# Causal grouped-query attention in a decoder kernel: scores taken twice, exponentials not transposed, sums of exponentials by additions and a product with ones

## The reference, cut to what matters

```python
q = (x @ Wq + bq).reshape(b, s, NQ, D); k = (x @ Wk + bk).reshape(b, s, NKV, D); v = (x @ Wv + bv).reshape(b, s, NKV, D)
q = _rotary(q); k = _rotary(k)
logits = jnp.einsum('bqhgd,bkhd->bhgqk', q.reshape(b, s, NKV, g, D), k) * scale
logits = jnp.where(causal, logits, jnp.float32(-1e+30))
w = jax.nn.softmax(logits, axis=-1)
out = jnp.einsum('bhgqk,bkhd->bqhgd', w, v).reshape(b, s, NQ * D)
return out @ Wo + bo
```

## Time and profile before

| | |
|---|---|
| median of three runs | 1377.93 us |
| profiled execution: its span, first to last instruction (it has no other time) | 1376.4 us |
| the changed stage, first to last scores | 350.4 to 948.4 us |
| TensorE busy in it | 582.84 of 598.00 us |
| VectorE, ScalarE, GpSimd busy in it | 323.18, 353.64, 193.77 us |
| mean granted TensorE clock, whole span | 0.939 of 2.4 GHz |

### The profile page before, as it was taken

One profiled execution on the slowest core, in us unless ns is written; L12 is line 12 of the kernel. 1 busy time (PEld: TensorE's weight loads), 2 busy tenths in 40 slices (PEclk: granted clock), 3 DMA queues, 4 the chain that ended last, 5 costly groups with the idle time before them and its releaser, 6 DMA issues. The chain is left out here.

```text
span 1376.4 us, 24979 instructions
## 1 busy us (share of the span) xinstructions
PE 1186.4 (86%) x8059; PEld 868.3 (63%) x8060; DVE 865.8 (63%) x1528; ACT 763.2 (55%) x2082; POOL 586.3 (43%) x616
## 2 busy tenths in 40 slices
PE   7888589676899999999999999999898439999991
PEld 4544367455566767777666777776676337888881
DVE  2588799874345545665355555675688666777773
ACT  2498447434555656666455565664366245565652
POOL 1155447656445331431553322200267415666663
PEclk9999789888699999999999999999999658999996
DMA  9100000001010010000100000100730232232325
GB/s 300 40 1 1 0 1 2 1 16 31 17 32 16 16 26 10 14 16 6 42 16 17 16 17 1 47 2 1 269 99 1 74 122 43 46 52 47 50 46 138
DMA packets 42136, 58.27 MB, mean 42 GB/s; under 512 B 6608, under 2 KB 34640, under 8 KB 42032
## 3 DMA queue, kind: packets, MB, share of 16 engines
q1 hardware_dynamic: 34544, 46.70, 11.3%
q0 software_dynamic: 7488, 10.23, 4.6%
HBM read 32.80 MB, written 13.63 MB: 34 GB/s over the span
## 5 line engine op out<-in xcount | busy, mean ns | idle before, releaser
L2016 DVE TENSOR_REDUCE ga_neg_top<-ps 128x1 f32<-128x128 f32 (+7 forms) x256 | 182.0, 753 | 195.2 <-PE ps L1786 194.8
L1897 ACT ACTIVATE ga_e<-ps,ga_neg_top 128x128 f32<-128x128 f32 (+7 forms) x256 | 188.4, 744 | 7.6 <-DVE ga_neg_top L2016 6.8
L1906 ACT COPY ga_e_tr<-ps 128x512 f32<-128x512 f32 (+3 forms) x192 | 92.2, 480 | 174.4 <-PE ps L1795 171.7
L1795 PE MATMUL ps<-ident,ga_e 128*128 128x128 f32 x1152 | 165.1, 278 | 0.9 <-DVE ga_e_tr L2024 0.8
L1811 PE MATMUL ps<-ga_e_tr,ga_v 128*64 128x256 f32 x1152 | 151.7, 391 | 4.1 <-ACT ga_att L1914 4.1
L1795 PEld LDWEIGHTS ps<-ident,ga_e 128*128 128x128 f32 x1152 | 123.3, 142 | 28.0 <-ACT ga_e L1897 14.7
L2024 DVE COPY ga_e_tr<-ps 128x128 f32<-128x128 f32 (+3 forms) x192 | 105.9, 552 | 35.1 <-PE ps L1795 34.8
L1971 POOL TENSOR_TENSOR ga_q_lo<-shared,ga_q_hi 128x1024 fp32r<-128x1024 f32 x15 | 35.6, 2370 | 176.1 <-ACT ga_q_hi L1887 176.1
L2566 DVE TENSOR_TENSOR ex_w_lo<-ex_gate_up,ex_w_hi 128x1024 fp32r<-128x1024 f32 x78 | 92.4, 1226 | 26.6 <-ACT ex_w_hi L2426 26.4
L1811 PEld LDWEIGHTS ps<-ga_e_tr,ga_v 128*64 128x64 f32 x1152 | 72.5, 136 | 49.0 <-issue 23.4
L2426 ACT CAST ex_w_hi<-ex_gate_up 128x1024 fp32r x78 | 77.9, 1046 | 23.7 <-issue 16.4
(11 more groups left out here) (330 smaller groups left out, 2721.4 us busy)
## 6 DMA issues: line engine op xcount, KB each, us to landing
shared<-shared SPq DMA_DIRECT2D x80, 128.0 KB, 2.3
ex_gate_up<-in_ex_gate_up SPq DMA_DIRECT2D x1, 8192.0 KB, 24.3
ex_down<-in_ex_down SPq DMA_DIRECT2D x1, 4096.0 KB, 35.7
x_tr<-in_x_tr SPq DMA_DIRECT2D x4, 512.0 KB, 7.0
x_nat<-in_x SPq DMA_DIRECT2D x1, 2048.0 KB, 11.7
gated_rows<-shared SPq DMA_DIRECT2D x8, 256.0 KB, 2.2
gated_rows<-x_tr SPq DMA_DIRECT2D x8, 256.0 KB, 2.3
x_tr<-summed_rows SPq DMA_DIRECT2D x8, 256.0 KB, 5.1
```

Source lines behind the costliest of these rows:

```text
L1795: last = nc.tensor.transpose(ps_tr[n % 2][:, (kb - k0) * P:(kb - k0 + 1) * P], e[half][t % 2][:, kb * P:(kb + 1) * P], core.ident[:])
L1897: nc.scalar.activation(e[half][t % 2][:, 0:blocks(t) * P], ps_scores(t, half), ACT.Exp, bias=neg_top[t % 2][:, half:half + 1], accum_out=s ...
L1906: nc.scalar.copy(e_tr[g % 2][:, k0:k1, half, t % 2 * P:(t % 2 + 1) * P], ps_tr[n % 2][:, 0:(k1 - k0) * P].rearrange("p (k t) -> p k t", t= ...
L2016: nc.vector.tensor_reduce(neg_top[t % 2][:, half:half + 1], ps_scores(t, half), AX.X, ALU.max, negate=True).then_inc(top_ready, 1)
```

## The change

The stage's ticks stay (now from -10 to 136), but inside them the work is cut anew. A **unit** takes, for a tile two places ahead (tile 1 aside), the scores queries x keys of the high parts only, up to 512 columns a half, adds the mask on the diagonal, and VectorE reduces it (up to 128x1024) to the negated maxima; there are 2, 4, 8, 8, 16, 16, 16, 16 units for n = 1 to 8. Once a tile the maxima are transposed (`turn_top`) and ScalarE writes them four times, masked (`spread_shift`). A **step** (J, c, kb) takes the scores again as keys x queries, for one block of 128 keys, four pairs of heads at once (512 columns): first a product that puts minus the maximum in every row, then the three split products, then on the diagonal the mask; there are 144 steps. ScalarE's exp of a step is one 128x1024 instruction; its output goes into `weigh_values` as it is. The exponentials of a group's steps are added up by VectorE (`add_keys`, 128x1024, 112 of them), and `sum_keys` multiplies the total with a [128, 64] matrix of ones (32 of them), which gives the sums already spread. VectorE inverts [128, 512] of them straight from bank 7 and multiplies. Queries are projected one tile earlier (three buffers), and one key piece at tick 8 instead of 16. On TensorE the work at the end of a tick stands in this order: output projection, transposed output, `turn_top`, `sum_keys`, query pieces, key pieces, value pieces. On ScalarE `spread_shift` follows the exponentials of its tick. The constants (`pair_rows`, `top_rows`, `ones`, `mask_k`) are made in the stage before.

```diff
-        self.recip_rows = sb("recip_rows", [P, P], F32R)
-        self.pick = sb("pick", [P, QT, 2, HD], F32R)
+        self.top_rows = sb("top_rows", [P, KV_PAIRS + R])
+        self.pair_rows = sb("pair_rows", [P, KV_PAIRS, P], F32R)
+        self.ones = sb("ones", [P, HD])
+        self.neg_top = [sb(f"neg_top{i}", [P, 2, HD]) for i in range(2)]
...
+    AHEAD, DRAIN = 10, 9
+    TICKS = range(-AHEAD, TICK_COUNT + DRAIN)
+    Q_BUFFERS, E_BUFFERS = 3, 4
+    steps = [(J, c, kb) for J in range(TILES) for c in range(KV_PAIRS) for kb in range(blocks(J))]
+    for s, (J, c, kb) in enumerate(steps):
+        place = (s - first_step[J]) * QT // (KV_PAIRS * blocks(J))
+        steps_at.setdefault(J * QT + place, []).append(s)
...
+    for J in range(TILES):
+        n_rows = max(1, PIECE // blocks(J))
+        own = [(J, c, r, r + n_rows, n) for c in range(KV_PAIRS) for r in range(0, R, n_rows) for n in range((blocks(J) - 1) // PIECE + 1)]
+        for i, unit in enumerate(own):
+            place = (J - 2) * QT + 6 + i * QT // len(own)
+            if J == 1:
+                place = 2 + i
...
-        return (J + 2, i - 6) if i >= 6 and J + 2 < TILES else None
-    K_STEPS = {1: 2 * QT, 2: 5 * QT, 3: 8 * QT}
+        return (J + 3, i - 6) if i >= 6 and 2 <= J + 3 < TILES else None
+    K_STEPS = {1: QT, 2: 5 * QT, 3: 8 * QT}
...
+    def top_turn_at(t):
+        J, i = divmod(t, QT)
+        return J + 1 if i == 6 and 0 <= J + 1 < TILES else None
+    def sums_at(t):
+        J, i = divmod(t, QT)
+        if i == 6 and 0 <= J < TILES:
+            return J * KV_PAIRS
+        if i == 1 and 1 <= J <= TILES:
+            return (J - 1) * KV_PAIRS + 1
+        return None
...
+                def top_scores(u):
...
+                    need(pe, top_ready, u)
+                    for r in range(r0, r1):
+                        for half in range(2):
+                            last = nc.tensor.matmul(ps_top[:, half, columns], q_hi[J % Q_BUFFERS][rows, c * R + r, :],
+                                                    k_hi[k_slot(b, n)][rows, c, 0:width], start=(r == r0), stop=(r == r1 - 1 and not diagonal))
+                    if diagonal:
+                        for half in range(2):
+                            whole = ps_top[:, half, 0:(r1 - r0) * width].rearrange("p (r k) -> p r k", k=width)
+                            last = nc.tensor.matmul(whole[:, :, width - P:width], ident_bf[:], mask_q[:].unsqueeze(1).to_broadcast([P, r1 - r0, P]),
+                                                    start=False, stop=True)
+                def turn_top(J):
+                    take_piece_bank((shift_ready, J + 1))
+                    pe.wait_ge(top_ready, last_unit[J] + 1)
+                    nc.tensor.transpose(ps_piece[:, 0:P], neg_top[J % 2][:].rearrange("p h x -> p (h x)"), core.ident[:]).then_inc(top_turned, 1)
+                def key_scores(s):
...
+                    need(pe, e_ready, s - 1)
...
+                    for half in range(2):
+                        last = nc.tensor.matmul(out(half), pair_rows[rows, c, :], shift[J % 2][rows, :, :], start=True, stop=False)
+                    for i, (ks, qs) in enumerate(((k_hi, q_hi), (k_hi, q_lo), (k_lo, q_hi))):
+                        for half in range(2):
+                            last = nc.tensor.matmul(out(half), ks[slot][rows, c, keys], qs[J % Q_BUFFERS][rows, heads, :],
+                                                    start=False, stop=(i == 2 and not diagonal))
+                    if diagonal:
+                        for half in range(2):
+                            last = nc.tensor.matmul(out(half), ident_bf[:], mask_k[:].unsqueeze(1).to_broadcast([P, R, P]), start=False, stop=True)
+                def weigh_values(s):
...
+                    pe.wait_ge(e_ready, s + 1)
...
+                    for half in range(2):
+                        last = nc.tensor.matmul(ps_att[half * HD:(half + 1) * HD, :], v[:, v_slot(b, kb), kv * HD:(kv + 1) * HD],
+                                                e[s % E_BUFFERS][:, half, :], start=(kb == 0), stop=(kb == j))
+                def sum_keys(g):
+                    take_piece_bank((recip_ready, g + 1))
...
+                    for half in range(2):
+                        last = nc.tensor.matmul(ps_piece[half * HD:(half + 1) * HD, :], ones[:], of_keys[:, half, :], start=True, stop=True)
...
+                for t in TICKS:
+                    for i in range(max(len(own_steps), len(own_units))):
+                        if i < len(own_steps):
+                            key_scores(own_steps[i])
+                        if i < len(own_units):
+                            top_scores(own_units[i])
+                        if i < len(own_steps) and own_steps[i] >= 1:
+                            weigh_values(own_steps[i] - 1)
...
+                    if top_turn_at(t) is not None:
+                        turn_top(top_turn_at(t))
+                    if sums_at(t) is not None:
+                        sum_keys(sums_at(t))
+                    if q_piece_at(t) is not None:
+                        take_piece_bank((piece_copied, piece["q", *q_piece_at(t)] + 1))
+                        front.pe_project_q(*q_piece_at(t), ps_piece)
...
+                def spread_shift(J):
+                    for r in range(R):
+                        last = nc.scalar.activation(shift[J % 2][:, r, :], ps_piece[:, 0:P], ACT.Copy, scale=top_rows[:, KV_PAIRS + r:KV_PAIRS + r + 1])
...
+                def exponentials(s):
...
+                    nc.scalar.activation(e[s % E_BUFFERS][:], ps_keys[s % 2], ACT.Exp).then_inc(e_ready, 1)
...
+                def find_maximum(u):
...
+                    nc.vector.tensor_reduce(out, ps_top[:, :, 0:(r1 - r0) * width].rearrange("p h (r k) -> p h r k", k=width),
+                                            AX.X, ALU.max, negate=True).then_inc(top_ready, 1)
...
+                def add_keys(s):
+                    before = e[(s - 1) % E_BUFFERS] if kb == 1 else added[g % 2]
+                    nc.vector.tensor_tensor(added[g % 2][:], before[:], e[s % E_BUFFERS][:], ALU.add).then_inc(add_ready, 1)
+                def normalise(g):
+                    dve.wait_ge(sums_ready, g + 1)
+                    nc.vector.reciprocal(recip[:], ps_piece).then_inc(recip_ready, 1)
+                    nc.vector.tensor_tensor(values, values, recip[:], ALU.mult).then_inc(att_done, 1)
...
+                    if sums_at(t - 1) is not None:
+                        normalise(sums_at(t - 1))
+                    for i in range(max(len(own_steps), len(own_units))):
+                        if i < len(own_steps) and own_steps[i] >= 1:
+                            add_keys(own_steps[i] - 1)
+                        if i < len(own_units):
+                            find_maximum(own_units[i])
```

More of the change, by code:

```diff
@@ L1624, in k_slot, with group, ends_group @@
+    def group(s):
+        return steps[s][0] * KV_PAIRS + steps[s][1]
+    def ends_group(s):
+        J, c, kb = steps[s]
+        return kb == blocks(J) - 1
+    adds_through = [sum(kb >= 1 for _, _, kb in steps[:s + 1]) for s in range(len(steps))]
+    tops_merged = [sum(blocks(i) > PIECE for i in range(J + 1)) for J in range(TILES)]
     def k_slot(b, n):
@@ new lines, in exponentials @@
+                def exponentials(s):
+                    act.wait_ge(s_ready, s + 1)
+                    before = s - E_BUFFERS
+                    if before >= 0:
+                        J, c, kb = steps[before]
+                        act.wait_ge(weighed, before + 1)
+                        if blocks(J) == 1:
+                            act.wait_ge(sums_ready, group(before) + 1)
+                        else:
+                            act.wait_ge(add_ready, adds_through[before + 1 if kb == 0 else before])
+                    nc.scalar.activation(e[s % E_BUFFERS][:], ps_keys[s % 2], ACT.Exp).then_inc(e_ready, 1)
@@ L2060, in _ @@
+                    if t == TICK_COUNT:
+                        add_keys(len(steps) - 1)
                         dve.wait_ge(q_lo_ready, TILES)
```

379 lines of the change are left out of this document (149 added, 230 removed).

## The result

The changed kernel takes **1566.86 us** (median of four runs, 1564.7 to 1569.02), the kernel before 1378.12 beside it (1376.24 to 1379.14). The ratio is **1.1376, 95% interval 1.136 to 1.1393**: slower by 188 us. The forecast was 1503 with a range of 1425 to 1570: right in direction and just inside the range, 64 us short.

What follows compares the result with a forecast made beforehand. TensorE's own work was taken as the bound, any new wait paid in full: -10 + 67 + 11 + 25 + 25 + 13 + 10 = +141, less 16 for overlaps, on 1376.4 gives 1501, as a median 1503 us; range 1425 to 1570.

Steps and rivals of the forecast that it cites:

- TensorE's work: Matmuls and transposes removed (308 us) against those added (300) in the stage: -8, taken as -10 us, bounds -25 to +5.
- (a): Tick 6, bank 7: `sum_keys` waits for ScalarE's copies, 20 us; 13 query pieces wait for the reciprocal, 47; sum 67.
- (b): Three key pieces at ticks 0 and 1 wait 3.65 us each at bank 7: 11 us.
- (c): Tick after `sum_keys`: VectorE does reciprocal and product before addition and maximum, stopping TensorE's units: 25 us in about ten tiles.
- (d): VectorE's two-SBUF-input additions contend with GpSimd instructions: 83 us of VectorE, 25 us put on TensorE (0 to 80).
- (e): Stage start: tile 0 needs its maxima first; about 17 us pass, +13 us net (8 to 18).
- (f): Half-clock stretches on TensorE after waits of 3.65 us: 1.7 us each, six of 13 charged, 10 us (0 to 25).
- (g): Constants made in the stage before, and the shorter drain: nothing, 1 us if not.
- Rival 3: TensorE's clock stays low long after each wait, 13 times 4 us lost: 1555 us; chance 0.12.
- Rival 2: VectorE becomes the bound, the GpSimd lock falling on each addition: 1546 us; chance 0.2.
- rival 1: VectorE's reciprocal of 512 columns is as fast as the multiplication (0.69 us): 1430 us; chance 0.08.
- Rival 4: Waits at bank 7 vanish and only TensorE's work counts, so the kernel is faster: 1363 us; chance 0.06.

Runs made afterwards that it cites:

- fillers: Changed kernel plus 14 bf16 products of 512 columns on TensorE behind `sum_keys` at tick 6, ahead of the query piece: 1537 us.
- kernel with a copy: Changed kernel with VectorE's reciprocal of the sums replaced by a copy of the same shape, the inversion left out: 1481 us.
- later pieces: Changed kernel with query pieces one tick later (ticks 7 and 0 instead of 6 and 7): 1568 us.
- late reciprocal: Changed kernel with the sums copied out of bank 7 by ScalarE and inverted by VectorE behind the tick's maxima and additions: 1540 us.
- halves: Changed kernel with copied sums inverted on VectorE in two 256-column parts over two ticks, maxima ahead of additions, turned maxima copied out of bank 7: 1469 us.
- quarters: Against the kernel with halves: the reciprocal in four parts of 128 columns, at most one behind each slot, the product as a fifth piece: 1469 us.

## Why the prediction was right in direction and 64 us short

Step by step, predicted against measured (us on TensorE, stage against stage):

| step | predicted | measured |
|---|---|---|
| TensorE's work | -10 | -15.1 |
| (a) `sum_keys` behind the spread maxima | 20 | 20.4, of it 18.5 the spread maxima |
| (a) query pieces behind the reciprocal | 47 | 49.8, of it 45.0 the reciprocal |
| (b) key pieces | 11 | 11.4 |
| (c), (d) units behind VectorE | 25 + 25 | 66.7, the start's among them |
| (e) to the first step | about 17 | 16.1 (347.6 to 363.7) |
| (f) clock | 10, at most 25 | **65.5** |
| (g) drain | 0 | 6.0 |

The rows don't add up to the sum: they count waits that the kernel before had too, and some of the start's twice. In the parts of the table of experiments the forecast's +125 was -10 of work, +125 of idle (with 16 taken off) and +10 of clock; measured are -15, +140.5 and +65.5. So of the 66 us that the stage is longer than forecast 55 are the clock.

**What held.** The reciprocal of 512 columns: 3357 ns against 3.35 us, extrapolated from rows of 16 and 32 columns, 16 times away from the nearest. With it came the bank waits, each at its place: 13 gaps of 3.46, 1.23 behind ScalarE's copies. Tiles 7 and 15 lost least (0.9 and some -4), as said; tiles 4, 5 and 6 lost 15.3, 13.3 and 13.8 and not 7 to 12. TensorE's work is near 580, not the busy time (653): the forecast's "busy near 575" had forgotten that the clock shows in it.

**What failed: step (f), the size of the clock term.** The forecast took one stretch of the trace before, one gap of 3.04 us with 3.5 us at half clock behind it, priced it at 1.7, and charged six of 13 gaps. The fillers measured 2.6 each, and all 13 do it: 34 us. The second half was not in the list at all: the units' waits (up to 5.57 us) are gaps as well, and 12 stretches behind them lost 33 by their place in the trace. The term should have been 29 stretches by 2.5 us, 73, less the 7.8 that the stage had before. Rival 3 named the mechanism at 52 us and a chance of 0.12; its size was nearest, its reason (the low clock outlasts the gap) right, though it too counted bank 7 alone. The Trainium skill (TensorE: Matmul & The Clock Gate, HAM oscillation) warns of waits of this length in every turn of a loop; on the tick-6 gaps the trace agrees with the rule, and the prediction had reckoned it at 27 and then gone by less than half of that.

**What was luck.** That 1567 lies inside the range, by 3 us, is owed to luck: the upper bound of 1570 was taken from rivals 2 and 3, each alone, and not from the forecast's own terms. The lower one, 1425, doesn't follow from its working either: no lock, no clock loss and TensorE's -25 give 1453, and only rival 1 comes near it.

**What was right by a wrong split: (c) and (d).** 50 together against 66.7 less the start's share (5.1 ending at 378.0, 1.3 at 351.0). The lock of (d) was put at 1.15 us for each of 72 GpSimd instructions, 83 us of VectorE. In the trace 12 of 112 additions are longer than 1.4 us, 13 us in excess; the products add 3, and the merges of 16 columns, which nobody had counted, add 8: six of eight take 1.2 to 1.9 us instead of 0.18, beside GpSimd's low parts (L1987). That is 24 us of VectorE, of which some 10 stand ahead of a unit's wait (an estimate from the excess of each). So most of the term was (c): 40 of the 66.7 us stand behind a reciprocal. The lock is small here by how the two engines happen to lie, not by itself: it is 36 us in the kernel with a copy, 40 with later pieces, 35 with the late reciprocal, 39 and 42 with halves and quarters.

**What the forecast had not seen** is that (a) and (c) cover each other. They were added. In fact the wait at bank 7 gives VectorE the time that it would otherwise take from the unit behind it: without the wait the units took 29 us more, some 18 of them without the lock's share, and the kernel stayed at 1568. In a sum this does no harm; for mending the kernel it is what matters.

Rival 2 (VectorE becomes the bound) was put on the lock falling on each addition, which it did not, but came true in places: the ticks behind the sums hold more VectorE work than TensorE work, and from halves to quarters nothing is won. Rival 1 (a cheap reciprocal, 1430) was measured with the copy: 1481, so even that kernel would have been 104 us slower than before. Rival 4 never had a footing.

Left open: no run takes the lock against GpSimd away, so what it costs TensorE, in the kernel with a copy above all, is read from the traces alone; the unit waits' share of the clock was not measured by itself, only by its place in the trace; the split of the gain between halves and the two edits run with them is a difference of runs; and an inversion on so few columns as before the change (one a head) was not tried.

## What to carry to other kernels

Count the gaps, not only their length: where TensorE is busy throughout, every wait of some 2 us or more that comes back in each turn of a loop can cost its own length and again 2 to 3 us by half clock, and waits that a unit's single buffer makes are gaps as much as those at a shared bank. A sum that is replicated over partitions to save transposes is inverted at full width (512 columns, 3.36 us, for what 16 columns did in 0.25): look at what the elementwise work behind a product with ones costs. And before a wait is removed, ask what it hides: here two of them, taken away, came back at the next instruction that waits for the same engine, in part because VectorE's instructions then lay beside GpSimd's.
